# Prologue of an attention and mixture-of-paths layer: statistics of both halves of batch 0 ahead of both normalisations, ScalarE for its transposed tokens, dummy matmuls at the outset

## The reference

```python
xn = layernorm(x)                              # mean and variance over the 256 channels
# attention, 16 heads of 16 channels, causal
q, k, v = split(xn @ Wq.T), split(xn @ Wk.T), split(xn @ Wv.T)
q, k = rope(q), rope(k)                        # rotation of channel pairs by position
attn = softmax(mask(q @ k.T / sqrt(16))) @ v
a = merge(attn) @ Wo.T
# nine paths, one chosen for each token
m = k0 * prev(xn) + k1 * xn + k2 * next(xn)
p = argmax(tanh(m @ Wo1 + bo1) @ Wo2 + bo2)
f = layernorm(xn + (m @ W1[p] + b1[p]) @ W2[p] + b2[p]) * gamma + beta
out = x + a + f
```

## Time and profile before

| | us |
|---|---|
| median of 3 runs | 777.78 |
| lowest and highest | 777.35 and 777.78 |
| profiled execution, its own time | 779.82 |
| its span | 778.1 |

### The profile page before, as it was taken

The page is one execution under the profiler, slowest core; times in us unless marked ns, Lnnn a source line. Parts: engine busy times, 40 slices in busy tenths (PEclk is TensorE's granted clock), DMA queues, the critical chain, the costliest instruction groups (busy, mean ns, idle before and its releaser), DMA issues.

```text
span 778.1 us, 12612 instructions
## 1 busy us (share of the span) xinstructions
PE 739.4 (95%) x4426; PEld 371.7 (48%) x4426; DVE 641.7 (82%) x1896; ACT 448.7 (58%) x780; POOL 288.3 (37%) x459
## 2 busy tenths in 40 slices
PE   3969999999999999999999999999999999999997
PEld 2512334354565544345465544445465554355544
DVE  4999899889898789888988789898988678878732
ACT  6332655765655654775646745675656565664673
POOL 2001123990615112893524213596243302130524
PEclk9967999999999999999999999999999999999999
DMA  7269050224613434112651615112570615200103
GB/s 243 96 180 172 16 114 6 69 83 110 109 15 63 102 92 78 53 61 82 113 78 28 137 57 113 32 50 73 123 109 2 123 42 102 45 2 2 29 1 82
DMA packets 40594, 59.98 MB, mean 77 GB/s; under 512 B 4830, under 2 KB 36847, under 8 KB 37651
## 3 DMA queue, kind: packets, MB, share of 16 engines
q1 hardware_dynamic: 36002, 54.38, 29.9%
q0 software_dynamic: 4224, 4.19, 4.2%
q10 hardware_dynamic: 304, 0.60, 0.2%
HBM read 42.04 MB, written 16.85 MB: 76 GB/s over the span
## 4 chain that ended last, share of the span: by engine, by line
PE 71%; DVE 10%; POOL 9%; ACT 5%; DMA 2%; issue 2%; SPq 1%; ACTq 0%; DVEq 0%; POOLq 0%
PE bank L1607 15%; PE bank L1588 14%; PE bank L1569 13%; PE bank L1550 7%; PE bank L1560 6%; PE bank L1635 3%; PE bank L1523 3%; POOL prob L1047 3%; PE bank L1512 2%; POOL raw L1026 2%; ACT prob L1172 2%; DVE piecemax L1395 2%; POOL turned L1024 2%; PE bank L1530 2%; PE bank L1617 2%
## 5 line engine op out<-in xcount | busy, mean ns | idle before, releaser
L1172 ACT ACTIVATE prob<-bank 128x512 f32<-128x512 f32 x576 | 324.6, 597 | 193.2 <-PE bank L1588 190.0
L1392 DVE CUSTOM_DVE_ANT_0 bank<-bank,causal_sb 128x384 f32<-128x384 f32 (+3 forms) x512 | 240.3, 512 | 32.8 <-PE bank L1569 32.0
L1569 PE MATMUL bank<-k_st,q_st 96*128 96x512 bf16 (+3 forms) x768 | 235.3, 337 | 9.6 <-DMA q_st<-scratch 4.8
L1047 POOL TENSOR_SCALAR_AFFINE_SELECT prob<-prob 128x256 f32<-128x256 f32 (+1 forms) x320 | 125.9, 430 | 290.3 <-ACT prob L1172 287.4
L1588 PE MATMUL bank<-q_st,k_st 98*128 98x512 bf16 (+3 forms) x768 | 211.0, 329 | 8.2 <-ACT prob L1172 5.6
L1395 DVE TENSOR_REDUCE piecemax<-bank 128x1 f32<-128x512 f32 x256 | 163.9, 682 | 18.5 <-PE bank L1569 18.1
L1607 PE MATMUL bank<-prob,v_sb 128*17 128x512 f32 (+3 forms) x1536 | 142.8, 492 | 0.0
L1569 PEld LDWEIGHTS bank<-k_st,q_st 96*128 96x128 bf16 x768 | 71.9, 98 | 134.7 <-DVE piecemax L1392 49.4
L1588 PEld LDWEIGHTS bank<-q_st,k_st 98*128 98x128 bf16 x768 | 69.5, 97 | 110.6 <-ACT prob L1172 54.3
L1560 PE MATMUL bank<-w_sb,mid 128*128 128x256 f32 (+1 forms) x320 | 83.7, 383 | 0.0
L1392 DVE DVE_READ_ACCUMULATOR2_ANT piecemax<- 128x1 f32 x512 | 72.0, 141 | 0.0
(11 more groups left out here) (87 smaller groups left out, 699.4 us busy)
## 6 DMA issues: line engine op xcount, KB each, us to landing
scratch<-parts SPq DMA_DIRECT2D x16, 768.0 KB, 3.8
q_st<-scratch SPq DMA_DIRECT2D x90, 128.0 KB, 6.9
k_st<-scratch SPq DMA_DIRECT2D x15, 384.0 KB, 4.7
z<-in_x SPq DMA_DIRECT2D x8, 512.0 KB, 4.3
mask<-chosen SPq DMA_DIRECT2D x16, 256.0 KB
z<-in_x POOLq DMA_DIRECT2D x8, 512.0 KB, 7.3
k_st<-scratch SPq DMA_DIRECT2D x15, 256.0 KB, 5.3
out<-z SPq DMA_DIRECT2D x7, 512.0 KB, 6.5
```

The costliest lines, as they stand in the source:

```text
L1047: nc.gpsimd.affine_select(out=d, in_=d, compare_op=ALU.is_ge, fill=0.0, base=0, pattern=pattern, channel_multiplier=-1).then_inc(masked, 1)
L1172: nc.scalar.activation(prob[:, place_of(G, i), :], ps[:, :], ACT.Exp, scale=float(DK) ** -0.5).then_inc(act_took, 1)
L1392: nc.vector.tensor_tensor_reduce(ps, ps, causal_sb[:, HALF - w:HALF], 1.0, NEG, ALU.add, ALU.max, to).then_inc(dve_took, 1)
L1569: nc.tensor.matmul(begin(("max", G, u))[:, 0:w], q_st[0:PARTS, G % STACKS, h, t * P:(t + 1) * P], k_st[0:PARTS, G % STACKS, h, k0:k0 + w], ...
```

## The change

Three things are done, all ahead of the first scores.

1. In the prologue's list the order becomes: stats and pow of half 0, stats and pow of half 1, norm of half 0, norm of half 1, both transposes of half 0, the projections. As both normalisations now follow each other directly and share `rt`, VectorE waits for the end of the first before it refines the second root.
2. In batch 0 ScalarE takes both chunks of the transposed tokens, in both halves. The third piece of ones moves behind its copy of chunk 1. A projection over chunk c now waits for the copy of chunk c alone, in every batch; before, each waited for both.
3. `keep_at_work` is called with 14 matmuls ahead of all other work of TensorE as well. They wait for the second of GpSimd's constants (L1005 makes the bfloat16 identity that they read).

```diff
     for half in range(2):
         head("stats", 0, 0, half)
         head("pow", 0, 0, half)
+    for half in range(2):
         head("norm", 0, half)
-        if half == 0:
-            turn(0)
+    turn(0)
     project(0, 0)
...
-        return "act" if name[2] == 0 else "dve"
+        return "act" if name[2] == 0 or name[:2] == ("xnT", 0) else "dve"
...
-        IDLE_MATMULS = 10
+        IDLE_MATMULS, FIRST_MATMULS = 10, 14
...
+        def xnT_copied(n, c, half):
+            return (act_took if taker(("xnT", n, c, half)) == "act" else dve_took), TOOK["xnT", n, c, half]
...
-                if what == "xnT" and name[2] == 0:
+                if what == "xnT" and taker(name) == "act":
                     copy_xnT(*name[1:])
-                    if name == ("xnT", 0, 0, 0):
+                    if name == ("xnT", 0, 1, 0):
                         set_ones(2)
...
             def normalize(n, half):
+                if n == 0 and half:
+                    dve.wait_ge(xn_ready, NTH["norm", n, 0])
                 norm_root(n, 0, half)
...
             def project_qk(c, n, qk, eo, half):
                 pe.wait_ge(wqk_loaded, 16)
-                pe.wait_ge(act_took, TOOK["xnT", n, 0, half])
-                pe.wait_ge(dve_took, TOOK["xnT", n, 1, half])
+                pe.wait_ge(*xnT_copied(n, c, half))
...
-            def keep_at_work():
+            def keep_at_work(count):
                 former = PL.before["S", 0, 1]
-                pe.wait_ge(act_took if taker(former) == "act" else dve_took, TOOK[former])
-                for _ in range(IDLE_MATMULS):
+                if count == IDLE_MATMULS:
+                    pe.wait_ge(act_took if taker(former) == "act" else dve_took, TOOK[former])
+                pe.wait_ge(consts_set, 2)
+                for _ in range(count):
                     nc.tensor.matmul(unit(("S", 0, 1))[:, :], ident_bf[:, :],
                                      ident_bf[:, None, :].to_broadcast([P, HALF // P, P]), start=True, stop=True)
...
+            keep_at_work(FIRST_MATMULS)
             for name in ORDER:
...
-                        keep_at_work()
+                        keep_at_work(IDLE_MATMULS)
```

More of the change, by code:

```diff
@@ L1323, in mix @@
                     dve.wait_ge(act_took, TOOK["xnT", n, 0, 1])
-                    dve.wait_ge(dve_took, TOOK["xnT", n, 1, 1])
+                    dve.wait_ge(*xnT_copied(n, 1, 1))
                     if n == 0:
@@ L1451, in _ @@
                     second_root(*name[1:])
-                elif what == "xnT" and name[2] == 1:
+                elif what == "xnT" and taker(name) == "dve":
                     copy_xnT(*name[1:])
@@ L1518, in project_v @@
                 pe.wait_ge(act_took, TOOK["xnT", n, 0, i // 2])
-                pe.wait_ge(dve_took, TOOK["xnT", n, 1, i // 2])
+                pe.wait_ge(*xnT_copied(n, 1, i // 2))
                 ps = begin(("v", n, i), m)
```

## The result

| | before | changed |
|---|---|---|
| median, us | 777.78 | 780.35 |
| executions timed | 20 | 20 |
| profiled execution, its own time | 779.82 | 781.28 |
| its span | 778.1 | 779.4 |

The ratio is 1.0024, with an interval of 1.0013 to 1.0036: slower by 2.6 us or 0.3% of the medians, outside the range and on the side with the smallest chance. The executions of the changed kernel scatter from 776.78 to 782.2. Those of before lie between 777.35 and 783.28, but for one of 850.63. Of the changed kernel 13 of the 20 lie above 779.5, and 3 of the 20 of before.

A forecast was written before the change was run, and what follows sets the result against it. TensorE was taken to set the pace from about 90 us, with VectorE's chain before it, so prologue gains count one for one. Between -0.1 and 0.8 us, 0.2 was taken off 777.78: 777.6, range 775.3 to 779.0.

The forecast's parts named there:

- the side with the smallest chance: Whole kernel: slower by more than 0.2%, 1.6 us; chance 0.10, against 0.25 for faster and 0.65 for same.
- Statistics first: Prologue: statistics of half 1 start at 8.3 us; transposes of half 0 come at 12.65 instead of 11.09.
- Copies by ScalarE: Prologue: VectorE saves a 0.6 us copy, then waits; "lo" comes 0.4 us later relative to the rotations.
- The clock at the outset: TensorE's prologue: whether the clock raised by the dummies falls before the projections; gain -0.1 to 0.8 us, or 2.3.
- (a): Prologue: the clock falls before the projections; 777.6 us, between 776.9 and 778.5; chance 0.65.
- (b): Prologue: the clock stays up from the dummies through the transposes; gain 2.3 us, 775.5; chance 0.18.
- So the shift reaches the maxima and the scores as it is: Behind the prologue: VectorE's chain is unbroken from "lo" to the store at 43.79, so the prologue's shift carries over unchanged.
- The dummies themselves cost nothing: Outset: TensorE idled for 11.09 us there, and the transposes queued behind are not due before 12.65; cost zero.
- The same order of instructions: Behind the prologue: the planner was expected to give the same order, as all engines' free times move together.
- rival (c): Later half-clock spell falls away or is added: 1.9 us less or more, 775.9 or 779.7; chances 0.07 and 0.05.
- Rival (d): Projections: the clock stays low longer; if all 16 passes run at half clock, 782.5 us; chance 0.05.

The follow-up runs named there:

- f1_first28: The changed kernel with 28 instead of 14 dummy matmuls at the outset; 782.30 us, ratio 1.0052 to before.
- e8_before_late: The kernel before with four small ScalarE copies ahead of its copy of the first shift, so the placing is issued later; 781.95 us, ratio 1.0046.
- ctl_after: The changed kernel repeated unaltered, on the chip of the runs that remove the late shift; 780.24 us, ratio 1.0015 to before.
- f4_act_mixed: The kernel before with ScalarE's copies and narrower wait alone, plus SyncE's second fill waiting for VectorE's third mixing step; 775.95 us, ratio 0.9980.
- f3_mixed: The changed kernel with SyncE's second fill waiting for VectorE's third mixing step; 780.33 us, ratio 1.0016 to before.
- f2_first7: The changed kernel with 7 instead of 14 dummy matmuls at the outset; 778.82 us, ratio 1.0017 to before.
- e1_dummies: The kernel before with only the third part, the 14 dummy matmuls at the outset; 778.41 us, ratio 1.0002.
- e2: The changed kernel without the 14 dummy matmuls at the outset; 777.67 us, ratio 1.0001 to before.
- e4: The kernel before with only the second part, ScalarE's copies and the narrower wait of the projections; 777.22 us, ratio 0.9990.
- e3: The kernel before with only the first part, the new order of statistics and normalisations with its wait; 779.04 us, ratio 1.0014.
- f5: The changed kernel with SyncE's second fill waiting for VectorE's fourth mixing step; 777.54 us, ratio 0.9991 to before.
- f6: The kernel before with ScalarE's copies and narrower wait alone, plus SyncE's second fill waiting for VectorE's fourth mixing step; 776.50 us, ratio 0.9989.
- e5: The changed kernel with SyncE issuing the second group's fill only when both placing transfers have landed; 777.49 us, ratio 0.9993 to before.
- e7: The kernel before with SyncE issuing the second group's fill only when both placing transfers have landed; 779.52 us, ratio 1.0016.
- e6_idle: The changed kernel with 24 instead of 10 idle matmuls behind the first shift, keeping TensorE busy over the gap; 779.01 us, ratio 1.0009 to before.
- e9_sp: The changed kernel with SyncE instead of ScalarE issuing both placing transfers, ahead of the second fill; 776.81 us, ratio 0.9997 to before.

## Why the prediction was wrong

The delay of the second fill behind the first placing transfer, over all profiled executions in which ScalarE places the shift and the second fill follows:

| kernel | fill behind placing, us | first scores behind copy, us |
|---|---|---|
| f1_first28 | -0.82 | 7.96 |
| changed | 0.80 | 6.59 |
| e8_before_late | 1.12 | 6.89 |
| ctl_after | 1.13 | 6.84 |
| f4_act_mixed | 1.39 | 7.12 |
| f3_mixed | 1.40 | 6.43 |
| f2_first7, e1_dummies | 1.46 | 4.38, 4.20 |
| before | 1.49 | 4.23 |
| e2, e4, e3 | 1.50, 1.50, 1.51 | 4.54, 4.30, 4.37 |
| f5, f6 | 2.58, 2.58 | 4.56, 4.21 |
| e5, e7 | 2.99, 3.53 | 4.57, 4.29 |

e6_idle (1.47) is left out, since its idle matmuls set the start of its scores. It is a step, not a slope: 1.40 is late by over 2 us, 1.46 is not. Before stood 0.03 to 0.09 us from it, and nothing in its trace says so.

By the prediction's own steps:

- **Statistics first: right.** 7.92 and 12.20 against 8.3 and 12.65; both loads of x landed earlier. The order alone puts "lo" 1.3 us later and the median 1.4 higher (e3_order), nearly one for one.
- **Copies by ScalarE: right.** VectorE idles 0.69 us before "lo", where about 1 was forecast. In e2_nofirst, with order and copies alone, "lo" is 0.2 us earlier than in before and the median is unchanged.
- **The clock at the outset: half right.** Both cases occur: the clock held over 2.60 us without work in one execution and fell within 3.33 in the other, about 2.2 us behind the last dummy (1.00 over 10 to 11 us, 0.51 over 11 to 12). Of the eight profiled executions with all three parts and 14 dummies it fell ahead of the projections in five and held in three (the changed kernel, e9_sp, f3_mixed). The chances of 0.65 and 0.18 were drawn from a single row of 2.9 us; for (a) this came near, for (b) it was low. The Trainium skill, TensorE: Matmul & The Clock Gate, § Seeing it yourself, with its fall 5.2 us after the last matmul, agrees with the first execution, whose gap between work was shorter, and not with the second. The size for (b) was right: 27.0 forecast for "lo", 26.67 measured.
- **"So the shift reaches the maxima and the scores as it is": this step failed.** The maxima came 2.6 us earlier and the copy of the shift 2.63, the first scores only 0.27. I followed VectorE's chain and took the transfers behind it to move rigidly with it. But the earlier trace rows ends with that store, 6.46 us of transfer, and I did not go on behind it. The first fill depends on its landing, which moved against the maxima by 0.3 to 0.7 us in the changed kernel, and the scores on a small transfer that races with the next fill.
- **"The dummies themselves cost nothing": failed with it.** I named only TensorE's idle time as cover. They take no time of any engine that matters; yet with order and copies in place the more there are, the more executions lie above 779.5: 1 of 12 without them, 20 of 32 with 14.
- **The same order of instructions: right**, on every engine, but for the edits of the prologue.
- **Later spells, rival (c): right mechanism, mis-sized.** It was priced at 3.8 us of half clock, 1.9 us, with a chance of 0.05 for the worse side. Measured are 17.0 us more between 55 and 105, and 5.3 us lost with the gap. Rival (d), priced at 782.5, did not happen: in neither profiled execution did all 16 passes run at half clock.

The late shift is worth what its removal gives: 780.24 to 777.49, 2.75 us (e5_place against ctl_after on one chip). The two intervals overlap a little, but that of the first comparison, 1.0013 to 1.0036, lies clear of e5_place's (up to 1.0009), and e9_sp and f5_mixed4, by two other routes, come to 776.81 and 777.54. e6_idle, whose scores start as late behind the copy but with matmuls in place of the gap, is 1.2 us below ctl_after and has no long half-clock spell in its trace; that this 1.2 is the clock's part is likely and not shown, as the two intervals overlap. With the late shift removed the changed kernel is level with before by the median (ratios 0.9993 and 0.9991, both intervals around 1), and not 2.6 us faster as "lo" was in the first trace. Part of that is the clock at the outset: it fell in the profiled executions of e5_place and f5_mixed4, with "lo" at 27.61 and 27.86, and held in that of e9_sp, with 26.65. How often it falls in the others is not known, so the size of this part stays an argument.

The best version is f4_act_mixed, 775.95: ScalarE's copies and a later second fill, in the old order and without dummies at the outset. It beats before by 0.2% [0.09, 0.32] and the changed kernel by 4.4 us of the medians, which come from different chips. It is the lowest of seventeen variants, which flatters it. In its profiled execution (779.76) the fill stands at 1.39, on the wrong side of the step; that its other executions are mostly on the right side I take from their times, and no trace shows it. f6_act_mixed4, safely beyond the step at 2.58, has 776.50, with an interval that contains 1.

Open: why e7_before_place is slower than before; why the store mostly lands earlier with dummies at the outset; why a late placing loses over 2 us and not some tenths; what makes the executions above 779.5 that remain without a late shift.

## What to carry to other kernels

An earlier start is worth nothing until every transfer between it and the bound is followed to its landing: list for each queue what is issued within 2 us of a small transfer that someone waits for, and read how near it is. Where two queues race, set their order by a wait, or issue both on one queue, before tuning what lies ahead of them. Look at the spread of executions beside the median: the share above one bound (1 of 12, 5 of 12, 20 of 32, 6 of 6) showed what no single trace does. Before such a count is read as a dose, repeat it on one chip: here it was not.

## What the hardware showed

- TensorE waited 2.35 to 3.19 us for a small DMA of the ScalarE queue in the six traces in which a large fill was issued on SyncE's queue between 0.82 us ahead of it and 1.40 us behind it. At 1.46 us or more behind it the first scores never waited for it. How much earlier the DMA then landed no trace shows.
- TensorE's clock fell from 2.4 to 1.2 GHz in a gap of 2.68 us (full at 53 to 55 us, 0.54 over the next 10), and in another place of the same execution held over one of 2.60 us; in e9_sp it held over 3.08. The half-clock spell behind the gap lasted 24 us, though TensorE was busy for 14.67 of the 15 us from 65 to 80.
- A store's landing was set by one DMA engine of 16 that worked up to 1.6 us longer than all others (before, 48.2 to 49.8 us). The tail differed between kernels, down to none in f1_first28, and between two executions of the same kernel: the fill stood at 5.96 and 6.30.
